# Attention scores from row halves of the array in place of stacked q and k

## What is computed

```python
qkv = normed @ W_qkv.T + b_qkv
q, k, v = (qkv[..., 0], qkv[..., 1], qkv[..., 2])
scores = jnp.einsum('bqhd,bkhd->bhqk', q, k)
scores = jnp.where(causal_mask, -jnp.inf, scores)
attn = jax.nn.softmax(scores, axis=-2)
z = jnp.einsum('bhqk,bkhd->bqhd', attn, v)
```

## Time and profile before

| | |
|---|---|
| median of three runs | 1500.27 us (1495.83 to 1503.83) |
| span of the profiled execution | 1498.5 us |
| TensorE busy | 1317.3 us, 88% |
| VectorE busy | 892.5 us, 60% |
| ScalarE busy | 596.9 us, 40% |
| score matmuls (L661) | 1536, 352.4 us busy |
| transfers into KS and QS | 384 of 256 KB |

### The profile page before, as it was taken

The page is one execution under the profiler, slowest core; times in us unless marked ns, Lnnn a source line. Parts: engine busy times, 40 slices in busy tenths (PEclk is TensorE's granted clock), DMA queues, the critical chain, the costliest instruction groups (busy, mean ns, idle before and its releaser), DMA issues.

```text
span 1498.5 us, 23566 instructions
## 1 busy us (share of the span) xinstructions
PE 1317.3 (88%) x6488; PEld 913.9 (61%) x6488; DVE 892.5 (60%) x2486; ACT 596.9 (40%) x1387; POOL 327.7 (22%) x487
## 2 busy tenths in 40 slices
PE   2699998999999999999999999999998846999996
PEld 0455555556566566565666666666664735888885
DVE  4466666666666766666666665666556561444443
ACT  1255555554544544454544444444444001111110
POOL 2121121112222322222222212121211341111111
PEclk7799999999999999999999999999999967999998
DMA  5656667545666656656655555565557882566540
GB/s 187 168 146 159 170 172 198 144 109 141 149 152 151 160 149 155 152 149 157 160 144 137 140 134 141 133 152 147 149 145 233 307 274 79 187 212 226 177 150 16
DMA packets 146223, 240.21 MB, mean 160 GB/s; under 512 B 15993, under 2 KB 77307, under 8 KB 145913
## 3 DMA queue, kind: packets, MB, share of 16 engines
q1 hardware_dynamic: 137608, 214.50, 53.9%
q10 hardware_dynamic: 4464, 16.25, 2.7%
q0 software_dynamic: 4096, 8.82, 1.6%
HBM read 94.76 MB, written 48.00 MB: 95 GB/s over the span
## 4 chain that ended last, share of the span: by engine, by line
PE 57%; SPq 12%; issue 10%; DVE 10%; DMA 6%; ACT 3%; POOL 1%; DVEq 0%; ACTq 0%; POOLq 0%
PE SC L661 12%; PE Z L673 8%; PE Z L821 8%; PE SC L795 8%; SPq L474 6%; PE XB L636 6%; PE XA L697 6%; PE XA L636 5%; DMA xp<-in_x 4%; DVE SC L1056 3%; ACT E L856 3%; PE XA L646 2%; PE XB L646 2%; SPq L531 1%; DVE nm L1056 1%
## 5 line engine op out<-in xcount | busy, mean ns | idle before, releaser
L1056 DVE CUSTOM_DVE_ANT_0 SC<-SC,mask 128x512 f32<-128x512 f32 (+7 forms) x512 | 380.0, 780 | 259.7 <-PE SC L661 259.4
L856 ACT ACTIVATE E<-SC,nm 128x512 f32<-128x512 f32 (+7 forms) x512 | 376.6, 739 | 380.6 <-DVE nm L1056 380.4
L661 PE MATMUL SC<-QS,KS 128*128 128x512 f32 (+3 forms) x1536 | 352.4, 366 | 19.9 <-DMA KS<-XK 14.0
L673 PE MATMUL Z<-E,vs 128*64 128x512 f32 (+3 forms) x1536 | 304.7, 503 | 59.0 <-DVE vs L1044 59.0
L661 PEld LDWEIGHTS SC<-QS,KS 128*128 128x128 f32 x1536 | 257.1, 196 | 98.4 <-issue 46.0
L673 PEld LDWEIGHTS Z<-E,vs 128*64 128x64 f32 x1536 | 85.4, 136 | 164.1 <-issue 78.4
L821 PE MATMUL Z<-W,hh 128*128 128x256 f32 x512 | 114.9, 383 | 2.2 <-DVE yb L1278 2.2
L795 PE MATMUL SC<-bT,W 128*128 128x256 f32 x512 | 115.0, 384 | 0.0
L1044 DVE TENSOR_TENSOR vs<-V,ri 128x128 f32<-128x128 f32 x256 | 92.7, 362 | 27.3 <-DVE ri L1038 1.1
L795 PEld LDWEIGHTS SC<-bT,W 128*128 128x128 f32 x512 | 98.7, 193 | 13.8
L821 PEld LDWEIGHTS Z<-W,hh 128*128 128x128 f32 x512 | 97.2, 192 | 15.6 <-DVE yb L1278 2.6
(11 more groups left out here) (193 smaller groups left out, 1782.9 us busy)
## 6 DMA issues: line engine op xcount, KB each, us to landing
KS<-XK SPq DMA_DIRECT2D x256, 256.0 KB, 4.6
QS<-XQ SPq DMA_DIRECT2D x128, 256.0 KB, 4.3
W<-in_w SPq DMA_DIRECT2D x32, 1024.0 KB, 8.5
z_s<-zs ACTq DMA_DIRECT2D x31, 512.0 KB, 4.0
zt<-z_s SPq DMA_DIRECT2D x24, 512.0 KB, 4.3
W<-in_wqk SPq DMA_DIRECT2D x33, 257.0 KB, 4.4
slots_s<-zt SPq DMA_DIRECT2D x16, 520.0 KB, 5.8
xb<-slots_s SPq DMA_DIRECT2D x16, 520.0 KB, 3.8
```

Of the source, the lines that this page charges most:

```text
L661: last = pe.matmul(SC[h][:, at:at + z - a], KS[:, ap, h, part, lo:lo + P], QS[:, ap, h, a:z], start=(part == 0), stop=(part == 1))
L673: last = pe.matmul(Z[DH * h:DH * h + DH, a:z], vs[:, kb % 2, DH * h:DH * h + DH], E[:, h, kb % 2, a:z], start=(kb == 0), stop=(kb == (3 if ...
L856: act.activation(E[:, h, kb % 2, lo:S], SC[h][:, at:at + S - lo], ACT.Exp, bias=nm[:, h, kb:kb + 1], scale=-1.0, accum_out=rs[:, kb, h:h + ...
L1056: dve.tensor_tensor_reduce(SC[h][:, at:at + S - lo], SC[h][:, at:at + S - lo], mask[:, 0:S - lo], 1.0, BIG, ALU.add, ALU.min, nm[:, h, kb: ...
```

## The change

Scores come straight from XQ and XK, now double-buffered by the step's parity. Head 0 lies on partitions 0 to 63 and so on the upper row half of the array, head 1 on the lower. For each span there are three products of 64 rows a head: hi k x hi q, hi k x lo q, lo k x hi q, and their order alternates between the heads. The product lo x lo is no longer computed. `stack`, QS, KS, `qk_in` and both waits for it are gone. `score` now does both heads of a block, and waits first for both heads' exponentials; the counts for both heads rise with the last pair of matmuls. A placeholder keeps the places of what lies behind in memory.

```diff
-        QS = sb("QS", [P, 2, 2, S], F32R, stack=att)
-        KS = sb("KS", [P, 2, 2, 2, S], F32R, stack=att)
-        XQ = sb("XQ", [P, 2, S], F32R, stack=att)
-        XK = sb("XK", [P, 2, S], F32R, stack=att)
+        XQ = sb("XQ", [P, 2, 2, S], F32R, stack=att)
+        XK = sb("XK", [P, 2, 2, S], F32R, stack=att)
+        sb("room_for_experts", [P, 8 * S], stack=att)
...
-            def stack(st, kind, half):
...
-                if st.has("proj"):
-                    sp.wait_ge(scores_done[1], st.n("scores"))
-                    settle(sp, sp_passed)
-                    stack(st, "q", 1)
-                    stack(st, "k", 0)
...
-                    stack(st, "k", 1)
...
-                def score(kb, h):
-
-                    pe.wait_ge(exp_done[h], st.of("expd", kb if kb <= 4 else kb - 1))
-                    if kb == 0:
-                        pe.wait_ge(qk_in[ap], qk_count(st))
+                def score(kb):
+
+                    for h in range(2):
+                        pe.wait_ge(exp_done[h], st.of("expd", kb if kb <= 4 else kb - 1))
                     lo = kb * P
                     spans = [(lo, HALF), (HALF, S)] if lo < HALF else [(lo, S)]
-                    for a, z in spans:
+                    for n, (a, z) in enumerate(spans):
                         at = a if kb < 4 else a - HALF + (kb % 2) * HALF
-                        for part in range(2):
-                            last = pe.matmul(SC[h][:, at:at + z - a], KS[:, ap, h, part, lo:lo + P],
-                                             QS[:, ap, h, a:z], start=(part == 0), stop=(part == 1))
-                    last.then_inc(scores_done[h], 1)
+                        for t, (kp, qp) in enumerate(((0, 0), (0, 1), (1, 0))):
+                            for h in range(2):
+                                rows = slice(DH * h, DH * h + DH)
+                                last = pe.matmul(SC[h][:, at:at + z - a], XK[rows, ap, kp, lo:lo + P],
+                                                 XQ[rows, ap, qp, a:z], start=(t == 0), stop=(t == 2))
+                                if n == len(spans) - 1 and t == 2:
+                                    last.then_inc(scores_done[h], 1)
...
-                        score(kb, 0)
-                        score(kb, 1)
+                        score(kb)
...
-                            act.wait_ge(qk_in[1 - pp], qk_count(st))
...
-                        act.activation(x[:, 0, half * HALF:(half + 1) * HALF], bank[:, :], ACT.Identity,
+                        act.activation(x[:, pp, 0, half * HALF:(half + 1) * HALF], bank[:, :], ACT.Identity,
...
-                                last = dve.scalar_tensor_tensor(XQ[:, 1, cols], bank[:, :], qkb[:, pp, 0:1],
-                                                                XQ[:, 0, cols].bitcast(F32), ALU.add, ALU.subtract)
+                                last = dve.scalar_tensor_tensor(XQ[:, pp, 1, cols], bank[:, :], qkb[:, pp, 0:1],
+                                                                XQ[:, pp, 0, cols].bitcast(F32), ALU.add, ALU.subtract)
```

More of the change, by code:

```diff
@@ L162, in settle @@
     eng.sem_inc(passed, 1)
-def qk_count(st):
-    return 12 * 16 * (st.b * PAIRS // 2 + st.j + st.pp)
 def zx_count(st):
@@ L354, in adaln_block @@
         wv_split = sem("wv_split")
-        qk_in = [sem(f"qk_in{k}") for k in range(2)]
         xln_in = [sem(f"xln_in{k}") for k in range(2)]
@@ L456, in _ @@
             sp.dma_start(woT[:, :, :], wo_d).then_inc(wo_in, 16)
-            def stack(st, kind, half):
[L461 to L464, removed]
-                    settle(sp, sp_passed)
-                cols = slice(0, S) if kind == "q" else slice(half * HALF, (half + 1) * HALF)
-                for h in range(2):
-                    rows = slice(DH * h, DH * h + DH)
-                    for part in range(2):
[L470 to L475, removed]
             def load_tail(st):
@@ L1076, in step @@
                             if kind == "q":
-                                last = dve.scalar_tensor_tensor(XQ[:, 1, cols], bank[:, :], qkb[:, pp, 0:1],
-                                                                XQ[:, 0, cols].bitcast(F32), ALU.add, ALU.subtract)
-                            else:
-                                last = dve.scalar_tensor_tensor(XK[:, 1, cols], bank[:, :], qkb[:, pp, 1:2],
-                                                                XK[:, 0, cols].bitcast(F32), ALU.subtract, ALU.subtract,
+                                last = dve.scalar_tensor_tensor(XQ[:, pp, 1, cols], bank[:, :], qkb[:, pp, 0:1],
+                                                                XQ[:, pp, 0, cols].bitcast(F32), ALU.add, ALU.subtract)
+                            else:
+                                last = dve.scalar_tensor_tensor(XK[:, pp, 1, cols], bank[:, :], qkb[:, pp, 1:2],
+                                                                XK[:, pp, 0, cols].bitcast(F32), ALU.subtract, ALU.subtract,
                                                                 reverse0=True)
```

## The result

| | before | after |
|---|---|---|
| median of four runs each, same chip | 1499.0 us (1495.83 to 1503.83) | 1512.8 us (1508.84 to 1515.64) |
| ratio after to before | | 1.0088 [1.0063, 1.0114] |
| span of the profiled execution | 1498.5 us | 1513.8 us |

The forecast was 1494. The result lies inside the range, with the wrong sign: 13.8 us lost where 7 were to be gained.

A forecast was written before the change was run, and what follows sets the result against it. It took TensorE, busy 88%, to be held by exponentials and, in blocks 4 to 7, by VectorE and ScalarE. 5.6 - 10.3 + 11.7 = 7 us off 1500.3 gave 1493.3, stated as 1494; range 1470 to 1532.

The forecast's parts named there:

- start: Before the first scores the idle for K goes, and their half pace: 10.2 + 1.5 = 11.7 us gained.
- steps with post: The 23 steps that have an output tile to finish: gains and losses by block sum to 5.6 us gained.
- steps without post: The 9 steps with no output tile to finish: block 1's scores wait longer; 1.14 x 9 = 10.3 us lost.
- Pairs and weight loads: Scores: a pair on row halves costs what one score matmul costs now, 0.23 us at 512 columns, 0.115 at 256.
- Rivals 2 and 3: Score pairs on row halves: weight loads don't run together, 1529 us, 15%; or pairs don't overlap at all, about 1600, 7%.
- Removed waits, zt: Block 0 with an output tile to finish: zt's load goes out some 8 us earlier, its wait goes; 15.2 us gained.
- The stagger: Both heads' scores end together and await both exponentials; block 1 loses 0.55 us with an output tile to finish, 1.11 without.
- Rival 5: The heads' common end costs half because VectorE has unseen slack: 12 us, 1482; 5%.
- The turns: Scores between whole-array work: switching into row halves costs 0.15 us, back 0.20; some 24 us in the sum.
- Rival 1: Switching the array to row halves for scores is nearly free: 24 us comes back, 1470; 15%.
- "Gain 0.4": Blocks 2 and 3 of the 23 steps with an output tile to finish: 0.4 x 23 = 9.2 us gained.
- rival 4: First scores of ten more steps with an output tile to finish start at 1.2 GHz, 1.5 us each: 1509; 8%.

The follow-up runs named there:

- e2: Changed kernel with three whole-array passes a span instead of row-half pairs, so no added turns; products sum over both heads, only time counts: 1486.2 us, 0.993.
- e1: Changed kernel with scores as before, head 0 then head 1 on the whole array, straight from XQ and XK, without stacking transfers: 1458.7 us, 0.974.
- v1: Changed kernel with VectorE's add of bo moved from block 1 to block 0: 1486.0 us, 0.993 of the kernel before.
- v3: v1 plus, in steps without post, q's second projection in block 0 and each half of k one block earlier: 1469.6 us, 0.981.
- v4: v1 plus the last value projection ahead of the weighting in its block, not behind it: 1476.0 us, 0.985.
- e3: e1 with the heads alternating, so both end together and both exponentials are waited for: 1512.7 us, 1.010 of the kernel before.
- e7: e1 with either head's scores waiting for both heads' exponentials, head 0 still ending halfway: 1467.9 us, 0.978 of the kernel before.

## Why the prediction was wrong

By its own steps, in us over the whole kernel:

| term | forecast | measured |
|---|---|---|
| start | 11.7 gained | 9.7 gained |
| steps with post | 5.6 gained | 0.2 lost |
| steps without post | 10.3 lost | 20.4 lost |
| from the last step on | nothing | 4.4 lost |

Of the start's 11.7, 1.5 are for the first scores' half pace. They lie inside the first step, so by this table's cut the forecast was 10.2 for the start and 8.8 lost in the steps without post.

- **Pairs and weight loads: right.** Pairs cost what one matmul did. Block 2's twelve matmuls, six of 256 and six of 512 columns, take 1.30 to 1.32 to the end of the last, and behind the turn its 256-column pairs start 0.12 apart. That leaves no room for 0.234 a pair. Rivals 2 and 3 are out. Rival 2's ground was true: a weight load of 64 rows takes 193 ns on the mean, and one of 128 rows took 196. But a pair doesn't pay for its two loads in turn.
- **Removed waits, zt: right.** K and xp are gone from the waits, and block 0 with post gained 18.0 us (forecast 15.2, over 23 steps). The start, by the same cut, is 0.5 short.
- **The stagger: mechanism right.** Block 1 without post starts at 5.72 (forecast 5.63), the projection held by bo 4.22 after block 1's scores (forecast 4.1), VectorE's first maximum at 1.86 (forecast 1.85). Rival 5 (it costs half) is out.
- **The turns: right in the sum, small for one.** A turn in was priced at 0.15, and both its ends together are 0.20, inside the bounds that were given, 0 to 0.23. For all added turns the sum held some 24 us, and by e2 they cost 24 to 26.5, with some of the clock in it: the next point shows a turn half hidden in a wait. So this term explains little of the miss. Rival 1 (turns nearly free) is out.
- **A failed step, the smaller one: "Gain 0.4" for blocks 2 and 3 with post.** The median block 2 of steps with post went from 4.65 to 4.62, block 3 from 4.41 to 4.27 in even and from 5.82 to 5.67 in odd steps: 0.03 and 0.15. The sum held the turn inside TensorE's stream, 4.45, and found the exponentials "just under it" at 4.38. They end at 4.48 (628.88 less 624.40), and the scores start 0.14 behind them: 4.62. e2, where nothing turns, shows what each part is. Its block 2 starts at 614.37:
```profile
614.37 1.21 PE L629 MATMUL SC<-XQ,XK 128*128 128x256 f32 x6
...
618.56 0.19 ACT L824 ACTIVATION_READ_ACCUMULATOR E<-SC,nm 128x1 f32 x1
...
618.89 1.27 PE L629 MATMUL SC<-XQ,XK 128*128 128x128 f32 x6
```
  Its exponentials end at 4.38, as the sum had it, and its scores start 0.14 later as well. So the 0.14 is not a turn: it stands between the exponential and the scores without one, and the sum left it out. What the turn adds is 0.10, the part behind its first pair; the part before the pair is hidden in the wait. The two blocks together fall 0.23 short of the gain, 5.3 us over 23 steps, most of what is missing from the steps with post.
- **The failed step that weighs most: the steps without post, "1.14 x 9 = 10.3 lost".** They lost 20.4. The undisturbed ones (odd) lose 1.64: block 0 and block 1 together 1.29 instead of 1.11 (the scores start 0.14 and not 0.07 behind the exponentials, and the turn delays them), blocks 2 and 3 give 0.20 back instead of 0.40, blocks 4 to 7 lose 0.55 instead of 0.43. And in five of the nine, block 1 is 7.0 long instead of 5.1, because its scores run at 1.2 GHz: the mean loss is 2.27. The sum left out that the wait which it did forecast ahead of block 1 can end at the low clock. The clock was rival 4, but sought in the first scores of steps with post, where it didn't move: 8 of 22 start so before and 8 after. It sits behind the wait that the change itself makes.
- **The tail** was costed at nothing. Its attention step is 1.4 longer; the last step has no projections beside which a chain of VectorE and ScalarE could lie. The other 3 are not explained: from the last step to the end, before, after and the ten experiments lie anywhere between 363.5 and 370.8.
- **The sign of being wrong** was that steps with post come under 34.5 or over 36. They came at 35.38, so it would have passed: it watched the steps that were nearly right, and not those without post. Of the 32% for "slower", 30 stood on rivals 2, 3 and 4, and none of them came as it was described.

The loss, split by the medians of the experiments: removed stacking -39 (before to e1), common end and doubled wait with one pass fewer +27.5 (e1 to e2), turns +26.5 (e2 to after). These are steps from kernel to kernel, so that they add up to the change is no check of them. The prediction had both large costs in its list and put them in the right places. Its benefit was short by some 10 us as well: it counted the waits that name a transfer, 28 us with the start, where e1 gained 39, a part of it by the clock.

**What the low clock is worth** can be read inside one trace, from the same block at both levels. In the changed kernel block 0 with post takes 8.08 on the mean where its scores start at 1.2 GHz (8 of 22) and 6.64 elsewhere; block 1 without post, behind a wait of about 2.46 in all but one step, takes 6.95 (5 of 9) and 5.13. That is 11.5 and 9.1 us. From the kernel's first scores to those of its last step TensorE is at 1.2 GHz for 43 us before, 58 after, 20.5 in e1, 27 in v1, 10 in v3 and 61 in v4. The kernels don't follow that order, because the waits differ too.

**Still open:** what makes such a block fall on the low clock, and so how many will in a kernel not yet run. Every experiment that moved their number moved a wait too.

## What to carry to other kernels

When two products are paired on the array halves, both end together: look first at who takes their results one after the other, and whether the chain behind the first was hidden by the second. In e3 this cost 54 us with not one matmul changed, twice what the turns cost by e2. If the pairing stays, move independent work of TensorE into the wait that it makes, and the instruction that frees a bank ahead of the delayed one; three such moves together turned 0.9% slower into 2.6% faster. Before crediting an edit with its whole gain, compare block by block: of v1's 27 us, 12 lay in a block that the granted clock had slowed.

## What the hardware did that was not expected

- A turn costs at both of its ends: 0.09 us before the first matmul in the new form and 0.11 behind it. Behind a wait only the second part shows: block 2 with post takes 4.62 in the changed kernel and 4.52 in e2.
- Where the scores wait for an exponential they start 0.14 us after its end, in the changed kernel as in e2, e3 and e7, where nothing turns there.
- Behind the same wait of 2.46 us TensorE runs at 2.4 GHz in one step of the changed kernel and at 1.2 GHz in another. Its windows there, with columns as in those of e3:
```profile
200.20:203.40 3.20, 3.20 (x20) 1.51 (x20) 2.00 (x5) 0.79 (x2) 0.16 (x1) 1.00 0.00 0
...
233.90:236.40 2.50, 2.50 (x12) 1.79 (x12) 0.42 (x2) 0.40 (x1) 0.04 (x1) 0.50 0.00 0
```
  Block 1's twelve matmuls, at 200.18 and 233.87 above, take 1.49 and 2.61. What sets the two apart the traces don't show.
- Taking 384 transfers of 256 KB out gained 25.7 us in the 22 steps with post and left their blocks 1 to 6 as they were, to 0.1 us each over all 22 steps. The traffic beside TensorE's, VectorE's and ScalarE's work in those blocks cost nothing that shows.
